# One list of steps per engine for the first three turns, one for the last two, and a new order of the loop

## What is computed

```python
# layer 0: masked attention with 6 heads of 64
q, k, v = heads(x @ Wq + bq), heads(x @ Wk + bk), heads(x @ Wv + bv)
probs = softmax(q @ k.T / sqrt(64) + where(adj, 0, NEG))
x = layernorm(x + (probs @ v) @ Wf + bf)
# layer 1: graph attention with 12 heads of 32
h = einsum('bnd,ade->bane', x, W)
attn = leaky(tanh(h) . w_src + (tanh(h) . w_dst).T)          # per head
f = elu(softmax(where(adj, attn, -999)) @ h + b)
gate = sigmoid(x @ H_w.T + H_b)
x = layernorm(x + gate * f + (1 - gate) * x)
```

## Time and profile before

| | |
|---|---|
| median of 3 runs | 1113.33 us |
| the profiled execution, its own time | 1116.9 us |
| its span, first to last instruction | 1114.9 us |
| PE busy | 1052.9 us, 94% of the span |
| DVE / ACT / POOL busy | 914.5 / 655.8 / 684.7 us |
| mean granted TensorE clock | 0.987 |

### The profile page before, as it was taken

The page is one execution under the profiler, slowest core; times in us unless marked ns, Lnnn a source line. Parts: engine busy times, 40 slices in busy tenths (PEclk is TensorE's granted clock), DMA queues, the critical chain, the costliest instruction groups (busy, mean ns, idle before and its releaser), DMA issues.

```text
span 1114.9 us, 28421 instructions
## 1 busy us (share of the span) xinstructions
PE 1052.9 (94%) x9199; PEld 898.5 (81%) x9199; DVE 914.5 (82%) x2289; ACT 655.8 (59%) x2060; POOL 684.7 (61%) x605
## 2 busy tenths in 40 slices
...
DMA packets 34722, 31.00 MB, mean 28 GB/s; under 512 B 15872, under 2 KB 34688, under 8 KB 34688
## 3 DMA queue, kind: packets, MB, share of 16 engines
...
## 4 chain that ended last, share of the span: by engine, by line
PE 74%; DVE 13%; issue 7%; ACT 3%; POOL 2%; SPq 1%; DMA 1%; DVEq 0%; ACTq 0%; POOLq 0%
PE p_bank L477 46%; PE t_bank L616 4%; DVE weights L934 4%; PE scores L539 4%; PE context L560 3%; PE context L630 3%; PE t_bank L548 3%; PE context L636 3%; PE t_bank L644 2%; PE t_bank L586 2%; PE t_bank L607 1%; ACT probs0T L721 1%; DVE xT L814 1%; PE t_bank L509 1%; DVE cT L814 1%
## 5 line engine op out<-in xcount | busy, mean ns | idle before, releaser
L1041 POOL TENSOR_TENSOR w_rows<-qwT,own_head 96x1536 fp32r<-96x1536 f32 x64 | 176.0, 2752 | 78.9 <-ACT qwT L777 78.8
L934 DVE SCALAR_TENSOR_TENSOR weights<-t_bank,pqw,clip 128x128 f32<-128x128 f32 x768 | 207.8, 342 | 14.1 <-PE t_bank L616 11.7
L1034 POOL TENSOR_TENSOR prod<-th,w_sd 128x768 f32<-128x768 f32 x64 | 117.3, 1832 | 130.9 <-ACT th L740 130.9
L712 ACT ACTIVATE probs<-masked,neg_max 128x128 f32<-128x128 f32 x384 | 148.7, 392 | 2.8 <-DVE neg_max L852 2.5
L477 PE MATMUL p_bank<-w_h,x1T 128*128 128x384 f32 x576 | 114.3, 343 | 9.5 <-DVE x1T L814 9.5
L1046 POOL TENSOR_TENSOR f_b<-f_raw,bias 128x384 f32<-128x384 f32 x64 | 68.4, 1068 | 85.3 <-DVE f_raw L949 85.3
L477 PE MATMUL p_bank<-w_v,xT 128*128 128x384 f32 x576 | 116.5, 346 | 0.8
L477 PE MATMUL p_bank<-w_g,x1T 128*128 128x384 f32 x576 | 115.7, 346 | 0.0
L477 PEld LDWEIGHTS p_bank<-w_h,x1T 128*128 128x128 f32 x576 | 102.0, 190 | 16.6 <-DVE x1T L814 13.3
L477 PE MATMUL p_bank<-w_f,cT 128*128 128x384 f32 x576 | 114.3, 342 | 0.8 <-DVE cT L814 0.6
L899 DVE TENSOR_TENSOR gate_sum<-p_bank,gate_bias 128x384 f32<-128x384 f32 x64 | 34.9, 546 | 95.7 <-PE p_bank L477 95.7
...
## 6 DMA issues: line engine op xcount, KB each, us to landing
...
```

The lines of the kernel that those rows point to most:

```text
L712: last = act.activation(probs0[:, k % 2, b, j * P:(j + 1) * P], masked[:, k % 2, b * PAIRS + j, :], ACT.Exp, bias=neg_max[:, b * PAIRS + j ...
L934: last = dve.scalar_tensor_tensor(out=weights[:, g % 2, n, :], in0=src[:, i * P:(i + 1) * P], scalar=pqw[:, g % 2, 0, n:n + 1], in1=clip[: ...
L1034: pool.tensor_tensor(prod[:], over_heads(th[:], 2), w_sd[:], ALU.mult).then_inc(s_prod, 1)
L1041: pool.tensor_tensor(w_rows[0:QW_ROWS, k % 2], over_heads(qwT[:, k % 2, 1, :].bitcast(F32), H1), per_head(own_head[:], P), ALU.mult).then_ ...
```

## The change

1. `first`, `second` (and `load`) become one list per engine, `*_BEGIN`; `drain` and `last` become one list, `*_END`. A row now has three numbers: name, `k`, and the turn counted from the list's own (`-1` is layer 0 of group 0 alone, `0` the turn after). In both lists the steps of neighbouring turns stand mixed.
2. The loop's lists are laid out anew. The steps are the same; their order differs.
3. Where the loop begins, PE waits once until the last two users of each pair of banks in `BEGIN` have been read (`banks_free`).
4. Two waits follow: `clip(k)` waits only for the `e` steps of its own two graphs, and the first `e` of each graph waits for the `clip` of its pair.

No instruction of the computation is added or taken away.

```diff
 PE_LOOP = [
-    ("x1T", 3), ("pv1", 1), ("h", 3), ("pT", 0), ("pT", 1), ("pT", 2), ("pT", 3), ("pv0", 0), ("s", 3), ("sumsT", 1),
+    ("pv1", 1), ("h", 3), ("pT", 0), ("s", 2), ("pT", 1), ("pT", 2), ("pT", 3), ("pv0", 0), ("s", 3), ("qwT", 2),
...
+FIRST, SECOND = ("begin", -1), ("begin", 0)
...
-def phases(eng, step, engine, NG):
-
-    for name, k in ORDERS["load"][engine]:
-        step(name, k, -2, "load")
-    for name, k in ORDERS["first"][engine]:
-        step(name, k, -1, "first")
-    for name, k in ORDERS["loop"][engine]:
-        step(name, k, 0, "second")
+def phases(eng, step, engine, NG, between=None):
+
+    for name, k, d in ORDERS["begin"][engine]:
+        step(name, k, d, ("begin", d))
+    if between:
+        between()
     with eng.Fori(1, NG - 2) as u:
-        for name, k in ORDERS["loop"][engine]:
-            step(name, k, u, "loop")
-    for name, k in ORDERS["drain"][engine]:
-        step(name, k, NG - 2, "drain")
-    for name, k in ORDERS["last"][engine]:
-        step(name, k, NG - 1, "last")
+        for name, k, d in ORDERS["loop"][engine]:
+            step(name, k, u, ("loop", d))
+    for name, k, d in ORDERS["end"][engine]:
+        step(name, k, NG - 2 + d, ("end", d))
...
+            def banks_free():
+
+                for freed in (t_freed, p_freed):
+                    for before, kb, db in bank_uses(freed, "begin")[-2:]:
+                        s, per = freed[before]
+                        te.wait_ge(s, upto(db + SHIFT.get(before, 0), per, kb + 1))
...
-                    wait(dve, s_e, upto(g1, THIRDS * GROUP, THIRDS * GROUP))
+                    wait(dve, s_e, upto(g1, THIRDS * GROUP, THIRDS * 2 * (k + 1)))
...
+                    if r == 0:
+                        dve.wait_ge(s_mx, upto(g1, 2, g // 2 + 1))
```

More of the change, by code:

```diff
@@ L41 @@
[L41 to L45, removed]
+    ("vout", 0), ("masks", 0), ("x1hi", 0), ("qkout", 0), ("qkout", 1), ("qkout", 2), ("hout", 0), ("x1hi", 1),
@@ L46 @@
 ]
 DVE_LOOP = [
[L48 to L52, removed]
[4 rows of a table removed]
@@ L57 @@
-    ("clo", 3), ("xlo", 0), ("mixb", 2), ("mv1", 1), ("gsum", 3), ("stats0", 2), ("x1", 1), ("xlo", 1), ("clip", 1),
-    ("mv0", 2), ("sum0", 3), ("stats0", 3), ("sum1", 2), ("xlo", 2), ("mv0", 3), ("xlo", 3), ("mixa", 3),
-    ("stats1", 2), ("out", 1), ("mv1", 2), ("mixb", 3), ("sum1", 3), ("stats1", 3), ("mv1", 3), ("x1", 2), ("out", 2),
+    ("x1lo", 0), ("gsum", 0), ("x1lo", 1), ("sd", 0), ("sda", 0), ("wlog", 0), ("qwlo", 0), ("sd", 1), ("sda", 1),
+    ("wlog", 1), ("qwlo", 1), ("gsum", 1), ("x1lo", 2), ("mask", 0), ("e", 0), ("max", 0), ("e", 1), ("e", 2),
@@ new lines @@
+    ("mask", 1), ("e", 3), ("e", 4), ("e", 5), ("rden0", 0), ("max", 1), ("rden1", 0), ("x1lo", 3), ("f_raw", 0),
+    ("sd", 2), ("sda", 2), ("rden0", 1), ("wlog", 2), ("gsum", 2), ("mask", 2), ("max", 2), ("sd", 3), ("sda", 3),
+    ("qwlo", 2), ("wlog", 3), ("mixa", 0), ("mixb", 0), ("qwlo", 3), ("sum1", 0), ("rden1", 1), ("clo", 0),
+    ("stats1", 0), ("mask", 3), ("mv1", 0), ("rden0", 2), ("f_raw", 1), ("max", 3), ("e", 6), ("e", 7), ("e", 8),
+    ("sum0", 0), ("stats0", 0), ("clo", 1), ("rden0", 3), ("mv0", 0), ("e", 9), ("e", 10), ("e", 11), ("mixa", 1),
```

282 lines of the change are left out of this document (165 added, 117 removed), and 79 rows, old and new, of tables (DVE_BEGIN, DVE_END, DVE_LOOP, PE_BEGIN).

## The result

The changed kernel takes 1104.26 us (median of 4 runs, 1102.80 to 1105.47), the kernel before 1113.32 us (4 runs, 1112.84 to 1113.53): a ratio of 0.9919, 95% interval 0.9901 to 0.9936. The gain is 9.1 us; I had forecast 21. The profiled execution took 1105.45 us, 1.2 us over its median; the one of before stood 3.6 us over its own. On other chips the kernel before ran from 1112.8 to 1119.0 us, the longer times mostly with a lower mean clock (0.982 against 0.989); so what follows compares ratios, or stretches of profiles, and gives the mean clock where two profiles differ in it.

A forecast was written before the change was run, and what follows sets the result against it. A loop turn was taken as 20.1 us of PE plus 45.9 us of DVE. Gains of 12.7 (end), 3.5 (beginning) and 4.5 us (loop) took 1116.9 to 1096.2 us, 1092 for the median; range 1079 to 1105.

The forecast's parts named there:

- The 36.5 us behind `x1T(3)`: End, after `x1T(3)` of turn 15: same work in one chain, so 36.5 us before and after, no gain.
- x1T(3): End, turn 15: starts 80.5 us behind `v(0)` of turn 14 instead of 93.2, gaining 12.7 us.
- the end yields half: Rival for the end: graph 3's chain through POOL stretches or the clock falls earlier; 6 us, not 12.7; 1099 us; chance 0.09.
- The base: Whole kernel: gains subtracted from the profiled 1116.9 us, 3.6 us over the median; 1096.2 us, or 1092 for the median.
- The beginning: Before the loop: mixing recovers 4.5 us of PE time, `banks_free` costs 1 us; net 3.5 us gained.
- The loop: Thirteen turns: listed moves sum to 0.0, 0.35 us a turn gained otherwise; 4.5 us in all, a turn 65.7 us.
- s(2): Loop, `s(2)` between `pT(0)` and `pT(1)`: fills PE's 0.7 us wait, but `mask(2)` on DVE waits; 0.6 us lost a turn.
- The ring: Loop: a turn is 20.1 us of PE plus 45.9 us of DVE; only shortening one of these shortens the turn.
- x_res: Loop, `x_res` behind both `rows` on POOL: frees `sda(0)` (2.24 us) and `wlog(0)` (1.77 us); gain hidden, allows early `qwT(0)`.
- qwT(0): Loop, `qwT(0)` before `qk(4)`: PE waits 0.2 to 0.5 us for `qkout(3)`; earlier `rows(0)` brings nothing.
- The rival of the other side: Loop: POOL's `prod(1)` holds `wlog(0)`, PE waits behind `qwT(0)`; 1.8 us a turn lost, 1120 us; chance 0.05.
- the rival at 1105: Loop gives some back: waits of `qk(4)` and `mask(2)` at their upper end, +0.6 us a turn, 8 us; chance 0.18.

The follow-up runs named there:

- old_end: Changed kernel with turns 14 and 15 unmixed, as before the change: ratio 0.9946 to the kernel before, median 1108.8 us.
- after_again: The changed kernel unedited, run again on the same chip as `old_end`: ratio 0.9890 to the kernel before, median 1103.0 us.
- before_waits: The kernel before with only part 4 of the change (the added waits): ratio 1.0034 to the kernel before, a turn 66.31 us.
- no_e_wait: Changed kernel without the added wait of the first `e` in the loop: ratio 0.9892 to the kernel before, a turn 65.65 us.
- s2_back: Changed kernel with the loop's `s(2)` back ahead of `wb(5)` on PE: ratio 0.9948 to the kernel before, a turn 66.31 us.
- old_loop: Changed kernel with the loop's lists of before: ratio 0.9973 to the kernel before, 1111.7 us, a turn 66.33 us.
- xres_early: Changed kernel with the loop's `x_res` back between `prod(0)` and `prod(1)` on POOL: ratio 1.0200 to the kernel before, 1138 us.

## Why the prediction was wrong

**The step that failed** is in the end: "The 36.5 us behind `x1T(3)` I leave as they are: the new order leaves the same work there". The work is nearly the same, 20.7 us of PE and 20.6 to 23.5 after. But `x1T(3)` came early by putting all of turn 14 beside turn 15, and so `wlog(2)`, `pqw(2)` and `sumsT(0)`, which in the old end were done ahead of `x1T(3)`, and `qwlo(2)`, which there took 0.27 us at the very end of `rows(1)`, now lie between `x1T(3)` and `h(3)`, beside POOL's `rows(1)`. At like clock the stretch cost 7.4 us more (`old_end` against `after_again`), where I had put nothing: 5.3 us ahead of `prod(3)`, of which 0.9 is `h(3)` at the low clock, and 2.2 us behind it. Avoiding two of the three holds gave back 1.5 us, since the third stood behind them; the remaining 6 us no run here took away. This is the chain of graph 3 through POOL that my rival *the end yields half* named, though the end yielded less than half. In the executions at the lower clock some 2 us more were lost behind `prod(3)`.

**x1T(3)** itself: forecast 80.5 us, measured 81.5. The working (DVE's 71.5 us of work plus the idle time at the head) held.

**The base.** I subtracted 12.7 us from an execution that took 3.6 us more than the median and whose clock was low in the last 17 us. At a clock like that of the later runs the old end left 34.5 us behind `x1T(3)`, not 36.5, and reached `x1T(3)` after 92.5 or 92.6, not 93.2 (`old_end`, and `before_waits`, whose turn 14 is in the old order too). Of the 21 us forecast, 2.7 were thus the state of the one execution that I started from.

**The beginning:** forecast 3.5 us gained and 1 us of wait in `banks_free`; measured 4.3 and 1.24. Right, the more as `v(0)` of turn 1 varies by itself, from 121.8 to 123.1 us in the runs with the new beginning. That this wait costs 2.38 us behind the old beginning I had not said.

**The loop:** forecast 65.7 us a turn, measured 65.80. The sum was near, but by luck. *The added waits* were missing from it: 0.27 us a turn in the old order, 0.14 in the new; without them (`no_e_wait`) the turn is 0.40 us shorter than before, where I had 0.35. But one term of mine alone is off by 1.1 us, so others must be off by about as much the other way, and which ones is not shown. *s(2)*: "Nothing gained on the ring, 0.6 lost" is wrong in its sign. DVE does wait for `s(2)`, 1.33 us, but the move gains 0.51 us a turn. The ring that I read in the old order is open in the new one. There `qk(0)` started 0.13 us behind the end of `xlo(3)`; now `xlo(3)` ends at 387.36, 0.26 us ahead of it, and PE has nothing to wait for there:

```profile
386.84 0.52 DVE L910 TENSOR_TENSOR xT<-t_bank,xT 128x384 fp32r<-128x384 f32 x1
...
387.62 0.48 PE L573 MATMUL p_bank<-xT,w_q 128*128 128x512 f32 x1
```

From there on a wait of PE counts in full (`s2_back`), and the one of DVE before `mask(2)` does not. DVE is not wholly off the path, though: its added waits still cost 0.14 us. I had priced all moves with the limits of the old order. Under equal waits the new order is worth 0.53 us a turn (`old_loop`). *x_res*: "both are free" holds, 0.18 and 0.17 us, and that its move allows the early `qwT(0)` holds at 2.0 us a turn. *qwT(0)*: "which nobody on the ring asks for" is wrong. The early `rows(0)` is out of the way of `qwlo(1)`; with `qwT(0)` put back a turn takes 1.8 us more. The wait for `qkout(3)` that I feared before `qk(4)` does not show: the only wait of PE that the profile lists in turn 5 is 0.2 us, for `pTo`.

**The rival of the other side** (POOL's instruction holds `wlog(0)`, 1.8 us a turn, 1120 us) did not come: `sda(0)` and `wlog(0)` were done by 400.20, before `prod(1)` at 401.99. Its mechanism and its order of price are right, for a hold by another instruction: `xres_early` shows 1.93 us of wait at `qwT(0)`, and the same hold decided the end of the program, one turn from where I looked for it.

The range, 1079 to 1105, holds the result, for another reason than the one that the rival at 1105 gave.
